# The last head's row sums taken from its tiles by ones-matmuls, a layer norm moved into the last attention step, and the first MoE weights loaded into the place of x transposed

## What is computed

```python
def _L0_attn_ref(x, wq, wk, wv, wo, ...):
    q = (x @ wq.T).reshape(Bx, Tx, N_HEADS, D_HEAD).transpose(0, 2, 1, 3)
    ...
    scores = jnp.einsum('bhtd,bhsd->bhts', q, k) * scale
    scores = LOGIT_SOFTCAP * jnp.tanh(scores / LOGIT_SOFTCAP)
    scores = jnp.where(mask[None, None], -jnp.inf, scores)
    attn = jax.nn.softmax(scores, axis=-1)
    out = jnp.einsum('bhts,bhsd->bhtd', attn, v)
    ...
    return out @ wo.T
x = _layernorm(x + _L0_attn_ref(x, ...), axis=-1)
x = _layernorm(x + _L0_ffn_ref(x, ...), axis=-1)
```

## Time and profile before

| what | us |
|---|---|
| three runs | 1084.98, 1086.15, 1086.78 (median 1086.15) |
| the profiled execution | 1092.47 |
| its span, first to last instruction | 1090.7 |
| PE busy in it | 1019.1 (93%) |
| DVE busy | 850.7 (78%) |
| ACT busy | 698.9 (64%) |
| POOL busy | 647.2 (59%) |

### The profile page before, as it was taken

How to read it: one execution, slowest core, us unless ns; L and a number is a source line. 1 busy time by engine, 2 the same in 40 slices (tenths; PEclk the granted TensorE clock), 3 DMA queues, 4 the chain that set the end, 5 groups by cost and what they waited for, 6 DMA issues and landing times.

```text
span 1090.7 us, 17557 instructions
## 1 busy us (share of the span) xinstructions
PE 1019.1 (93%) x6072; PEld 809.2 (74%) x6072; DVE 850.7 (78%) x1391; ACT 698.9 (64%) x1162; POOL 647.2 (59%) x660
## 2 busy tenths in 40 slices
PE   7799999999999999999999999999999968899966
PEld 5588878887888788888878887888788747345532
DVE  6579898989898889888988898889988865833423
ACT  4667777777777777777777777777777752323212
POOL 2536666666666666666666666666666662365332
PEclk9999999999999999999999999999999987999987
DMA  5610011101110101010101000100000007739937
GB/s 193 238 30 20 31 39 30 62 30 39 31 61 30 41 30 61 31 40 30 62 30 40 31 20 30 40 30 20 21 20 21 21 1 227 209 86 265 237 55 235
DMA packets 52168, 75.42 MB, mean 69 GB/s; under 512 B 8208, under 2 KB 43248, under 8 KB 51952
## 3 DMA queue, kind: packets, MB, share of 16 engines
q1 hardware_dynamic: 48144, 69.30, 20.1%
q0 software_dynamic: 3072, 4.46, 2.2%
q10 hardware_dynamic: 864, 0.54, 0.2%
HBM read 63.00 MB, written 15.75 MB: 72 GB/s over the span
## 4 chain that ended last, share of the span: by engine, by line
PE 67%; DVE 16%; issue 6%; DMA 6%; POOL 2%; ACT 2%; SPq 0%; ACTq 0%; DVEq 0%; POOLq 0%
PE ps L462 19%; PE ps L463 18%; PE ps L464 18%; DVE prob_lo L1230 6%; PE ps L499 5%; DMA acc_rows<-ye,acci 4%; PE ps L676 2%; DVE qraw L1299 2%; POOL pacc L1089 2%; PE ps L720 2%; PE ps L767 1%; DVE qraw L1317 1%; DVE kT_lo L1230 1%; PE ps L716 1%; DVE qhat_lo L1230 1%
## 5 line engine op out<-in xcount | busy, mean ns | idle before, releaser
L1230 DVE TENSOR_TENSOR prob_lo<-praw,prob_hi 128x1024 fp32r<-128x1024 f32 (+7 forms) x256 | 301.4, 1201 | 3.4 <-ACT prob_hi L837 3.4
L1072 POOL TENSOR_SCALAR_AFFINE_SELECT praw<-praw 128x128 f32<-128x128 f32 x256 | 119.5, 467 | 264.4 <-ACT praw L893 261.6
L1089 POOL TENSOR_TENSOR pacc<-pacc,praw 128x768 f32<-128x768 f32 (+2 forms) x192 | 234.6, 1222 | 27.7
L887 ACT ACTIVATE praw<-ps,rk 128x1024 f32<-128x1024 f32 (+7 forms) x256 | 186.2, 741 | 68.8 <-PE ps L464 64.6
L837 ACT ACTIVATE prob_hi<-praw 128x1024 fp32r<-128x1024 f32 (+7 forms) x256 | 168.7, 686 | 1.9 <-POOL praw L1072 1.9
L893 ACT ACTIVATE praw<-praw 128x1024 f32<-128x1024 f32 (+7 forms) x256 | 168.2, 684 | 0.0
L462 PE MATMUL ps<-qhat_hi,kT_hi 128*128 128x512 f32 (+3 forms) x384 | 135.2, 352 | 9.6 <-DVE qhat_lo L1230 9.6
L462 PE MATMUL ps<-prob_hi,vS_hi 128*128 128x512 f32 (+3 forms) x384 | 136.4, 355 | 8.0 <-DVE prob_lo L1230 8.0
L463 PE MATMUL ps<-prob_lo,vS_hi 128*128 128x512 f32 (+3 forms) x384 | 133.9, 349 | 0.0
L464 PE MATMUL ps<-prob_hi,vS_lo 128*128 128x512 f32 (+3 forms) x384 | 133.0, 346 | 0.0
L463 PE MATMUL ps<-qhat_lo,kT_hi 128*128 128x512 f32 (+3 forms) x384 | 132.9, 346 | 0.0
(11 more groups left out here) (167 smaller groups left out, 2240.2 us busy)
## 6 DMA issues: line engine op xcount, KB each, us to landing
qsq<-rq_rows SPq DMA_DIRECT2D x32, 512.0 KB, 4.0
wgu<-in_wgu SPq DMA_DIRECT2D x16, 704.0 KB
wd<-in_wd SPq DMA_DIRECT2D x16, 352.0 KB
acc_rows<-acc_rows SPq DMA_DIRECT2D x8, 544.0 KB, 6.1
acc_rows<-pacc SPq DMA_DIRECT2D x8, 512.0 KB, 9.8
accA<-acc_rows SPq DMA_DIRECT2D x8, 512.0 KB, 5.8
wraw<-in_wqkv SPq DMA_DIRECT2D x15, 256.0 KB, 4.5
wvraw<-in_wqkv SPq DMA_DIRECT2D x16, 128.0 KB, 2.7
```

The source lines that it names most:

```text
L887: nc.scalar.activation(praw[:, raw_at(b, j)], buf[:, P * j:T], ACT.Tanh, scale=rk[:, b, j:j + 1]).then_inc(tanh_done, 1)
L1072: nc.gpsimd.affine_select(out=diag, in_=diag, compare_op=ALU.is_ge, fill=0.0, base=0, pattern=[[1, P]], channel_multiplier=-1).then_inc(ma ...
L1089: nc.gpsimd.tensor_tensor(pacc[:, P * j:T], before, raw, ALU.add).then_inc(pacc_done, 1)
L1230: v.tensor_tensor(dst, x_, hi.bitcast(F32), ALU.subtract).then_inc(done, 1)
```

## The change

1. **Row sums.** In the tail `sums` is replaced by `last_sums`. It reads the 8 masked tiles of step 31 straight from `praw`: for each tile four matmuls with ones as stationary operand, which accumulate in PSUM. That is 32 matmul instructions in place of 4, with 256, 224, ... 32 columns instead of 256 (1152 columns in each of the four strips in place of 256). POOL no longer accumulates step 31.
2. **Layer norm of batch 0.** In step 31 DVE takes its 8 statistics between tile 5 and the values `vc`, and aggregates them after tile 7 of step 30. POOL computes the reciprocal deviation after the mask of tile 3 of step 31. In the tail DVE normalises two of the 8 row tiles after each of the tiles 4 to 7.
3. **Layer norm of batch 1.** DVE takes two statistics after each output unit, each time after a wait for its own output of that unit.
4. **Weights.** The tensors `gwT`, `wsgu`, `wsd` and the first slots of `wgu` are declared first, so that they lie in the place of x transposed (`xT`). SP starts them once PE is done with the last unit that reads `xT` (`vc` of step 31): router and shared weights and the `wgu` of 4 pairs. The write of batch 0's rows follows, then the wait for `UNITS_ALL`, then the rest.

```diff
-            sp.wait_ge(pj_free, UNITS_ALL)
+            sp.wait_ge(pj_done, Step(NP_ - 1, 3, "last").unit("vc")[0])
...
-            for p in range(WR):
-                if p in (1, 3):
-                    b = p // 2
-                    sp.wait_ge(x1_done, b + 1)
-                    sp.dma_start(x1_v[:, TT * b:TT * b + TT, 0:D], yacc[:, TT * b:TT * b + TT, :]).then_inc(x1_out, 16)
+            for p in range(IN_XT):
+                gate_weights(p)
+            sp.wait_ge(x1_done, 1)
+            sp.dma_start(x1_v[:, 0:TT, 0:D], yacc[:, 0:TT, :]).then_inc(x1_out, 16)
+            sp.wait_ge(pj_free, UNITS_ALL)
+            for p in range(IN_XT):
+                down_weights(p)
+            expert_weights(IN_XT)
+            sp.wait_ge(x1_done, 2)
+            sp.dma_start(x1_v[:, TT:NT, 0:D], yacc[:, TT:NT, :]).then_inc(x1_out, 16)
+            for p in range(IN_XT + 1, WR):
                 expert_weights(p)
...
+            def last_sums(count, bank_no):
+
+                open_unit(count)
+                pe.wait_ge(mask_done, B * H * TT)
+                for j in range(TT):
+                    by_strip = strips(praw[:, raw_at(1, j)])
+                    for g in range(BLK):
+                        last = mm(ps[32 * g:32 * g + 32, bank_no, 32 * j:32 * TT].rearrange("p (j r) -> p j r", r=32), ones[:, :],
+                                  by_strip[:, g], start=j == 0, stop=j == TT - 1, tile_position=(0, 32 * g))
+                last.then_inc(pj_done, 1)
...
-            for j in (6, 7):
-                mask(B * H - 1, 1, j)
-            for j in range(TT):
-                accumulate(B * H - 1, 1, j)
...
+            s = B * H - 1
+            mask(s - 1, 0, 6)
+            mask(s - 1, 0, 7)
+            for j in range(TT):
+                accumulate(s - 1, 0, j)
+            for j in range(TT):
+                mask(s, 1, j)
+                if j == 3:
+                    layernorm_rstd(0)
...
+                if ending:
+                    dve.wait_ge(pj_free, Step(NP_ - 1, 2, "last").unit("op3")[0])
+                    tile_stats(0, TT)
...
-            dve.wait_ge(pj_free, Step(NP_ - 1, 3, "last").unit("op3")[0])
-            for n, j in enumerate((4, 5, 6, 7)):
+            dve.wait_ge(rln1, 1)
+            for j in (4, 5, 6, 7):
                 tile(s - 1, 1, j)
-                tile_stats(TT * n // 4, TT * (n + 1) // 4)
+                for i in (2 * j - 8, 2 * j - 7):
+                    ins = normalise(i)
+            ins.then_inc(x1_done, 1)
             output_lo(s - 1)
-            layernorm_stats(0)
             summed(1, *end.unit("sums"))
             for u in range(4):
                 out_projected(1, 1, u, s - 1, *end.unit(f"op{u}"))
-            dve.wait_ge(pj_free, UNITS_ALL)
...
+                dve.wait_ge(pj_free, end.unit(f"op{u}")[0])
+                tile_stats(TT + 2 * u, TT + 2 * u + 2)
+            layernorm_stats(1)
+            dve.wait_ge(rln1, 2)
+            for i in range(TT, NT):
+                ins = normalise(i)
+            ins.then_inc(x1_done, 1)
```

More of the change, by code:

```diff
@@ L41 @@
 WR = 8
+IN_XT = 4
 XD = D + E
@@ L223, in block_kernel @@
         att.close()
+        gwT = sb("gwT", [P, KC, E])
+        wsgu = sb("wsgu", [P, KC, 2 * SI])
+        wsd = sb("wsd", [P, 3, D])
         wgu = sb("wgu", [P, WR, 2, KC, 2 * FI])
@@ L228, in block_kernel @@
         xg = sb("xg", [P, PAIRS, XD])
-        gwT = sb("gwT", [P, KC, E])
-        wsgu = sb("wsgu", [P, KC, 2 * SI])
-        wsd = sb("wsd", [P, 3, D])
         silu_s = sb("silu_s", [P, SR, 512])
@@ L662, in _ @@
                 values(s - 1, 1, j)
-            sums(s - 1, 1, *end.unit("sums"))
+            last_sums(*end.unit("sums"))
             for u in range(4):
@@ L1134, in _ @@
                     step(Step(p, q, "middle"))
-            for q in range(STEPS):
+            for q in range(STEPS - 1):
                 step(Step(NP_ - 1, q, "last"))
-            for j in (6, 7):
-                mask(B * H - 1, 1, j)
-            for j in range(TT):
-                accumulate(B * H - 1, 1, j)
             def layernorm_rstd(b):
@@ L1408, in split_output_weights, with counted, settle, tile_stats @@
                 split(wo, (ALL, e), woraw[:, e], wohi_done, st.pair * 2 + e + 1, wolo_done)
+            steps = [0]
+            def counted(ins):
+                steps[0] += 1
+                ins.then_inc(dstep, 1)
+            def settle():
+                dve.wait_ge(dstep, steps[0])
+            def tile_stats(i0, i1):
+                for i in range(i0, i1):
+                    counted(v.bn_stats(stats[:, i, :], yacc[:, i, :]))
+            def layernorm_stats(b):
+                settle()
+                for i in range(TT * b, TT * b + TT):
+                    counted(v.bn_aggr(mv[:, i, :], stats[:, i, :]))
+                settle()
+                v.tensor_scalar(lnv[:, TT * b:TT * b + TT], mv[:, TT * b:TT * b + TT, 1], LN_EPS, None, ALU.add).then_inc(var1, 1)
+            def normalise(i):
+                return v.tensor_scalar(yacc[:, i, :], yacc[:, i, :], mv[:, i, 0:1], lnr[:, i:i + 1], ALU.subtract, ALU.mult)
             def opening(st):
@@ L1428, in step @@
                     projected("q1", 1 - k, s + 1, *st.unit("q1"))
+                ending = st.last and st.q == 3
                 if old:
@@ L1436, in step @@
                     tile(s - 1, 1 - k, 7)
+                if ending:
+                    layernorm_stats(0)
                 if new:
@@ L1520, in _ @@
                 out_projected(1, 1, u, s - 1, *end.unit(f"op{u}"))
-            dve.wait_ge(pj_free, UNITS_ALL)
[L1522 to L1525, removed]
-                dve.wait_ge(rln1, b + 1)
-                for i in range(TT * b, TT * b + TT):
-                    ins = normalise(i)
-                ins.then_inc(x1_done, 1)
+                dve.wait_ge(pj_free, end.unit(f"op{u}")[0])
[5 more added lines that the diff above has]
+            ins.then_inc(x1_done, 1)
             dve.wait_ge(consts, CONSTS)
```

26 lines of the change are left out of this document (6 added, 20 removed).

## The result

The changed kernel takes 1074.57 us (median of 4 runs, 1074.11 to 1075.78) where the kernel before took 1086.47 (4 runs, 1084.98 to 1094.52). The ratio is 0.9883 with a 95% interval of 0.9848 to 0.9918; repeated later beside 11 runs of the kernel before it was 0.9882 (0.9865 to 0.9898). The sign and the main mechanism were right, the size was too small by a third.

What follows compares the result with a forecast made beforehand. A single file of hand-overs from POOL's last additions to the logits was taken as the bound. Logits 8.7 us earlier, less 0.2 for the last step, gave 8.5: median 1086.15 to 1077.6, 8-in-10 range 1074.8 to 1080.8.

Steps and rivals of the forecast that it cites:

- the row sums: PE's ones-matmuls over the last head's tiles: 3.3 us, between bounds of 2.3 and 3.9, ending at 893.6.
- the stretch from ACT's first copy to the last logits: From ACT's copy of turned rows to PE's last logits: 17.15 us instead of 17.6, logits ending 8.7 us earlier.
- Tile 7: Last head's tile 7 on DVE: 0.3 us instead of 1.50 without POOL's additions, ending 1.25 us earlier.
- the step behind them: From the end of the sums to DVE's first output addition: 1.25 us, so that addition starts 6.4 us earlier.
- The rival with logits' price: Narrow sums cost 0.109 us a record like logits, 7.0 us or 14.0 at half clock; 1088.7 us, chance 0.04.
- The units: Four output units with a wait and two statistics between them: 1.73 us each, costing 2.0 of the 6.4 us.
- the first rival, the clock that stays up: PE idles less and keeps its high clock from ACT's first copy to the logits: 1074.7 to 1076 us, chance 0.14.
- The last step: Batch 0's eight new statistics, 2.71 us, fit DVE's 2.61 us idle time; 0.2 us charged, bounds 0 and 0.5.
- What is late next: Batch 1's normalisation is done at 908.3, PE wants the rows at 911.15: 2.8 us to spare.
- The early weights: 4 MB moved by 885 beside the last step at no charge; the 0.3 us wait for the weight load falls away.
- The distance from the logits to the end: From the last logits to the kernel's end: unchanged; a change of more than 2 us would show the forecast wrong.
- The rival in which normalisations meet POOL: Batch 0's normalisations between tiles 4 to 7 slow down beside POOL's masks: 1079 to 1081 us, chance 0.15.

Runs made afterwards that it cites:

- with PE busy the kernel before: The kernel before with 45 matmuls on the identity that nobody reads, 30 before the last head's sums, 15 after its output units; ratio 0.9981.

## Why the prediction was wrong in size

The reading of the place held: one file of hand-overs, the gain measured at the logits, POOL's sum as the main wait. What failed is two terms of the sum: the row sums, taken at 3.3 us (2.17 came, all of it hidden), and the stretch from ACT's first copy to the last logits, taken at 17.15 with the clock as before (14.97 and 16.63 came). Step by step, on the profile's clock and less the 0.4 us that the execution was ahead:

- *Tile 7*: 0.3 and 1.25 earlier were forecast; 0.28 and 1.25 came.
- *The row sums* were the term that was mis-sized first. 3.3 us were taken, "nearer to the upper bound because the weight loads of small groups don't shrink with the columns"; they took 2.17, just under the lower bound of 2.3, so the time goes by columns. The premise is so: each of the 64 records of a weight load is 0.11 us long, whatever the columns. But 64 of them make 7.0 us and all of it took 2.17: the loads run beside the matmuls and beside each other. With 2.17 the sums end before `oT_lo` does, and cost nothing; the forecast had 1.1 us of them on the path. With the step behind them, the first addition came 1.1 us earlier than forecast.
- *The price of a narrow record.* By the start times in the trace the records come in groups of four, one for each strip, and each of the eight tiles has two such groups, since a matmul is recorded as two. From one group to the next it takes:

  | columns | 256 | 224 | 192 | 160 | 128 | 96 | 64 |
  |---|---|---|---|---|---|---|---|
  | us to the next group of four | 0.216 | 0.189 | 0.163 | 0.136 | 0.109 | 0.083 | 0.056 |

  (Only the very first group takes more, 0.240.) That is 0.84 to 0.88 us for 1000 columns, with next to no constant part, and 0.014 us a record at 64 columns. The rival with logits' price (0.109 us a record) is out. The 62 ns a matmul of the Trainium skill (TensorE: Matmul & The Clock Gate, Back-to-back issue gap, with hardware decoding off) don't hold here either: two records are one matmul, so at 64 columns a matmul costs 0.028 us. Whether hardware decoding is off in these runs, no run shows. The forecast had also set the 62 ns against each of 64 records; by the 32 matmuls the rule gives 2.0 us as an estimate, which the total of 2.17 alone would not have refuted.
- *The units*: 1.73 us each was forecast, 1.58 came, because 0.75 is the record of two overlapping statistics, which cost 0.67, and the wait for DVE's own result costs 0.03, not 0.1. 0.5 us over three units.
- *The stretch from copy to logits*: 17.15 was forecast to the end of the last logits; 14.97 and 16.63 came in two executions (15.09 and 16.76 in the table, which goes to DVE's copy). This was the first rival, the clock that stays up, and it was held apart from the forecast as a case of its own with 0.14. Two executions of one program have it in part and in full, so it is less a case than a scatter. From copy to slots the forecast has 61.4 and the two executions 60.5 and 60.7; the better part of what a high clock gives before the logits is lost behind them, where a low stretch comes instead.
- *The last step* held: 0 us, with 2.70 us of statistics in 2.61 us of idle time, and so did the early transfers beside it: from 848 to the start of tile 7 the two executions differ by 0.04 us. *What is late next* held too: PE didn't wait for batch 1, though the rows were ready at 906.29 for transposes at 907.50, 1.2 us ahead and not 2.8.
- *The early weights*: 0.3 us was right alone (1.0003) and badly wrong as the worth of the part. With batch 0 normalised early, the late load is the next wait, 4.98 us in one trace and 5.05 in another. The forecast had the sum right, because it took both edits at once, but its sentence that the weights are worth 0.3 would have led anyone to leave them out.
- *The distance from the logits to the end* was to be what it was, within 2 us. By the spans it fell from 163.7 to 159.9 and 159.2. This is no effect of the change: 4.6 us of it are the longer chain of scatters in the one trace of the kernel before from which the forecast was made, and with PE busy the kernel before has 159.9 too.

The sum: sums and hand-over 1.1, units 0.5, copy to slots 0.8, and the 0.2 charged to the last step that was not there, 2.6 us at the slots. The rest of the miss, 12 against 11.1, is within what single medians of this kernel scatter. The range was too narrow for it by 0.2 us: it put the sums' lower bound and the high clock into a rival with a chance of its own, though both point the same way. What it set against the high clock did not hold. The units were to keep PE busy for well under half of their time; the second-last one kept it busy from 894.27 to 895.24, 0.97 us of 1.56, and the clock read 1.00 through all of them. And the second low stretch did come with the narrow logits, but with the last ones, near the point to which the gain was counted and behind it.

The rival in which normalisations meet POOL didn't take place in the changed kernel: the four pairs took 0.72 to 0.73 each, two of them with a mask of POOL beside them. It took place in the run with the norms alone, at 4.12 us for two, where POOL was adding up. That agrees with the rule of the shared port pair in the Trainium skill (SBUF — State Buffer, SBUF: two separate sides).

## What to carry to other kernels

Ask of every part of a change what it is worth alone, and what it is worth when the others are in: here the new sums gave nearly 10 us alone, the norms cost 4 and the weights gave nothing, yet taking the early weights out of the finished kernel cost 9. An operation that moves to an engine that was waiting is free as long as it ends before the other thing that engine waits for; so look up that cover's end before you size the operation. Don't build a forecast on the clock of one stretch in one execution: take the time between two points that are far enough apart to hold the low stretch wherever it falls. And before you take one profiled execution as the base, ask why it is slower than the median: here 4.6 us of it lay in one chain of scatters.

## What the runs showed of the hardware

Narrow matmuls side by side in four strips, with 32 stationary columns, cost by their columns, down to 0.014 us a record at 64 columns, with weight loads of 0.11 us each hidden beside them; the logits' records, with 128 stationary columns and 32 moving ones, cost 0.109. One and the same program ran the same four-matmul unit in 3.60 and in 5.30 us in two executions, and ten executions of one kernel spread over 10 us (1078.31 to 1088.40). Two layer norm instructions of DVE took 4.12 us beside POOL's additions and 0.73 beside its masks. The chain of dependent scatters came in two lengths, 89.7 to 89.8 and 94.3 to 94.4 us from slots to the load behind it, in the fourteen profiled executions. Where matmuls on the identity kept PE at work until a load landed, the first two records behind it took 1.02 us instead of 2.07; where PE still idled 5.80 us before the load, they took 2.08.
